# Output product from high and low parts, and a new order of VectorE and ScalarE behind the edge loop of a graph and attention layer

## The reference, cut to what matters

```python
m = v * attn[..., None]
out = jax.ops.segment_sum(m, dst, num_segments=n).reshape(n, H * D)
out = out @ Wo.T + bo
out = node_feat + out
mean, var = out.mean(axis=0), jnp.mean(jnp.square(out - mean), axis=0)
out = (out - mean) * jax.lax.rsqrt(var + EPS) * gamma + beta
...
kv = jnp.einsum('bhnd,bhne->bhde', kf, v)
z = jnp.einsum('bhnd,bhd->bhn', qf, kf.sum(axis=2))
out = jnp.einsum('bhnd,bhde->bhne', qf, kv) / (z[..., None] + EPS)
y @ w_proj + b_proj
...
x = x + gnn(xn, ...) + mix(xn)
x = x + ffn(_layernorm(x))
```

## Time and profile before

| | |
|---|---|
| median of 3 runs | 1625.43 us (1623.97 to 1627.98) |
| profiled execution | 1634.06 us, its span 1632.3 us |
| TensorE busy | 1547.8 us, 95% of the span |
| VectorE busy | 1253.1 us, 77% |
| ScalarE busy | 1053.7 us, 65% |
| GpSimd busy | 692.7 us, 42% |
| granted TensorE clock, mean | 0.985 of full speed |

### The profile page before, as it was taken

The page is one execution under the profiler, slowest core; times in us unless marked ns, Lnnn a source line. Parts: engine busy times, 40 slices in busy tenths (PEclk is TensorE's granted clock), DMA queues, the critical chain, the costliest instruction groups (busy, mean ns, idle before and its releaser), DMA issues. The chain is left out here.

```text
span 1632.3 us, 27290 instructions
## 1 busy us (share of the span) xinstructions
PE 1547.8 (95%) x7330; PEld 1200.3 (74%) x7334; DVE 1253.1 (77%) x3141; ACT 1053.7 (65%) x3706; POOL 692.7 (42%) x722
## 2 busy tenths in 40 slices
PE   7999897999999999999999999999999999999996
PEld 6886676777777777777777777777777776777663
DVE  5877654777787888888888778887888787678877
ACT  4775122667777777777777777777777776567244
POOL 1001123455555556555555565555555554211001
PEclk9999999999999999999999999999999999999997
DMA  5574415566666666666676666666676665175101
GB/s 193 182 242 180 178 64 154 179 214 194 213 204 208 228 210 216 208 201 197 205 237 214 206 214 204 214 208 204 213 219 207 201 211 175 54 226 178 37 14 51
DMA packets 135446, 300.31 MB, mean 184 GB/s; under 512 B 34863, under 2 KB 56502, under 8 KB 135296
## 3 DMA queue, kind: packets, MB, share of 16 engines
q0 software_dynamic: 63600, 180.17, 33.1%
q1 hardware_dynamic: 66512, 107.59, 22.2%
q10 hardware_dynamic: 5184, 10.81, 1.7%
HBM read 271.40 MB, written 66.58 MB: 207 GB/s over the span
## 5 line engine op out<-in xcount | busy, mean ns | idle before, releaser
L1110 ACT ACTIVATE wv<-vv,expd 128x64 f32<-128x64 f32 x1248 | 314.5, 334 | 2.8
L1122 ACT ACTIVATE old<-old,expd 128x64 f32<-128x64 f32 x1232 | 302.1, 334 | 0.0
L1032 POOL DMA_INDIRECT merge<-new,put_id x157 | 162.4, 1035 | 280.7 <-DVE new L1455 247.2
L1884 PE MATMUL psK<-M_hi,efT_hi 128*128 128x512 f32 x628 | 253.6, 404 | 2.8 <-ACT efT_hi L1080 2.8
L1884 PE MATMUL psV<-M_hi,efT_hi 128*128 128x512 f32 x628 | 255.9, 407 | 0.0
L1885 PE MATMUL psV<-M_lo,efT_hi 128*128 128x512 f32 x628 | 249.7, 398 | 0.0
L1885 PE MATMUL psK<-M_lo,efT_hi 128*128 128x512 f32 x628 | 249.2, 397 | 0.0
L1003 POOL DMA_INDIRECT old<-merge,dst_id x157 | 158.6, 1010 | 139.3 <-DMA merge<-new,put_id 109.2
L1096 ACT ACTIVATE expd<-diff 128x32 f32<-128x32 f32 (+1 forms) x79 | 18.1, 229 | 293.5 <-DVE diff L1434 293.5
L1003 POOL DMA_INDIRECT kv<-kv_table,src_id x157 | 160.7, 1023 | 66.1 <-issue 47.4
L1003 POOL DMA_INDIRECT qc<-q_table,dst_id x157 | 154.9, 987 | 55.7 <-issue 46.6
(11 more groups left out here) (323 smaller groups left out, 3323.5 us busy)
## 6 DMA issues: line engine op xcount, KB each, us to landing
first_ef<-in_ef_turned_dram SPq DMA_DIRECT2D x39, 512.0 KB
efT<-in_ef_turned_dram SPq DMA_DIRECT2D x39, 512.0 KB
merge<-empty ACTq DMA_DIRECT2D x4, 2640.0 KB, 9.7
rows<-merge SPq DMA_DIRECT2D x40, 256.0 KB, 3.8
row_block<-dst_rows POOLq DMA_DIRECT2D x13, 768.0 KB, 5.9
dst_line<-dst_rows SPq DMA_DIRECT2D x78, 128.0 KB
end_line<-end_rows SPq DMA_DIRECT2D x78, 128.0 KB
kv_table<-kv_out SPq DMA_DIRECT2D x10, 512.0 KB, 3.2
```

What stands on the lines that cost most here:

```text
L1032: pool.indirect_dma_start(out=merge[2 * (p % 2) + u][:, :], out_offset=bass.IndirectOffsetOnAxis(ap=put_id[:, t:t + 1], axis=0), in_=new[p ...
L1110: act.activation(wv[:, u, h * DH:(h + 1) * DH], vv[p % 2][:, u, h * DH:(h + 1) * DH], ACT.Copy, scale=expd[p % 2][:, u, 0, h:h + 1]).then_ ...
L1122: act.activation(rows, rows, ACT.Copy, scale=expd[p % 2][:, u, 1, h:h + 1]).then_inc(old_scaled, 1)
L1884: pe.matmul(out[:, :], efT_hi[b][:, u, c, :], Me_hi[:, c, col:col + D], start=c == 0, stop=False)
```

## The change

1. **Output product.** `Wo` and the transposed `g` are split into high and low parts in float32r, and each plain product of `output` becomes three products. The high part of `g` is made by `copy_g`, the low part by a new VectorE subtraction `turned_g_low` at the head of tile t for tile t-3. The high part of `Wo` is made by ScalarE at the end of its tile 8, the low part in two halves on VectorE in tiles 8 and 9. `turn_g` and `output` now wait for the low part.
2. **Place for them.** The scaled tables are written over `rows`; `part` is gone. SP may load the rows of tile t only when `g` of tile t-2 is made.
3. **VectorE's tile.** `add_parts` of tile t-1 moves from the end of tile t to its head, ahead of the minimum `before_exp`.
4. **ScalarE's tile.** `copy_v(t)` moves from the head of tile t+1 into the middle of tile t, between the two scaled tables.
5. **Division.** ScalarE takes the upper four heads of y (`weigh_half`), VectorE the lower four. In ScalarE's program `weigh_half(t+1)` stands ahead of `copy_y(t)`.
6. **Last stage.** On ScalarE `row_sd` goes ahead of `whole_numbers`, and `scale_y` goes behind it, one round later.

```diff
         wsc = sb("wsc", [P, 2, 2])
+        with ExitStack() as over_output:
+            Wo_lo = sb("Wo_lo", [P, C, D], F32R, where=over_output)
         Wo = sb("Wo", [P, C, D])
         with ExitStack() as over_queries:
...
+            with ExitStack() as over_ternary:
+                Wo_hi = sb("Wo_hi", [P, C, D], F32R, where=over_ternary)
             w_ffn = sb("w_ffn", [P, 2, 2 * D], where=sums_only)
...
-            sp.dma_start(Wo[:, :, :], WoT.rearrange("(c p) o -> p c o", p=P)).then_inc(Wo_in, 16)
+            sp.dma_start(Wo[:, :, :], WoT.rearrange("(c p) o -> p c o", p=P)).then_inc(w_in, 16)
             for t in range(2, NT):
-                sp.wait_ge(part0_done, 2 * (t - 1))
-                sp.wait_ge(act_parts, 2 * H * (t - 1))
-                sp.wait_ge(pool_part, t - 1)
+                sp.wait_ge(g_done, t - 1)
                 load_rows(t)
             sp.wait_ge(v_done, NT)
...
-                                   bc(scl2[:, t, 3, :], DH), ALU.mult).then_inc(pool_part, 1)
+                of_heads = rows[:, u, 3, :].rearrange("p (h e) -> p h e", e=DH)
+                pool.tensor_tensor(of_heads, of_heads, bc(scl2[:, t, 3, :], DH), ALU.mult).then_inc(pool_part, 1)
             pool.wait_ge(v_done, NT)
             pool.memset(res[:, NT - 1, :], 0.0).then_inc(cst, 1)
...
 
-            def parts(t):
+            def scale_table(t, i):
                 u = t % 2
                 act.wait_ge(scaled, 1 if t < 2 else 2)
                 act.wait_ge(rows_in[u], 16 * (TABLES + 1) * (t // 2 + 1))
-                if t >= 2:
-                    act.wait_ge(g_done, t - 1)
-                for i in (1, 2):
-                    for h in range(H):
-                        act.activation(part[:, u, i, h * DH:(h + 1) * DH], rows[:, u, i, h * DH:(h + 1) * DH], ACT.Copy,
-                                       scale=scl2[:, t, i, h:h + 1]).then_inc(act_parts, 1)
+                for h in range(H):
+                    of_head = rows[:, u, i, h * DH:(h + 1) * DH]
+                    act.activation(of_head, of_head, ACT.Copy, scale=scl2[:, t, i, h:h + 1]).then_inc(act_parts, 1)
 
             def copy_v(t):
...
             for t in range(NT):
-                if t >= 1:
-                    copy_v(t - 1)
                 exp(len(QJ) + t, D)
                 if t == 1:
                     table_exp(1)
-                parts(t)
+                scale_table(t, 1)
+                copy_v(t)
+                scale_table(t, 2)
                 if t >= 2:
                     copy_g(t - 2)
-            copy_v(NT - 1)
+                if t == 8:
+                    act.wait_ge(w_in, 64)
+                    act.wait_ge(summed_w, 5)
+                    act.activation(Wo_hi[:, :, :], Wo[:, :, :], ACT.Copy).then_inc(w_high, 1)
             copy_g(NT - 2)
             act.wait_ge(kv_added, NT)
...
             act.wait_ge(cst, 4)
+            def weigh_half(t):
+
+                u = t % 2
+                act.wait_ge(z_done, t + 1)
+                act.wait_ge(g_turned, NT)
+                if t >= 2:
+                    act.wait_ge(y_turned, t - 1)
+                for h in range(H // 2):
+                    act.activation(y[:, u, (H // 2 + h) * DH:(H // 2 + h + 1) * DH], ob[u][1][:, h * HW:h * HW + DH], ACT.Copy,
+                                   scale=z[:, t, 1, H // 2 + h:H // 2 + h + 1]).then_inc(y_half, 1)
+
+            weigh_half(0)
             for t in range(NT):
+                if t + 1 < NT:
+                    weigh_half(t + 1)
                 copy_y(t)
                 if t % 3 == 0:
...
+                if i < NT:
+                    row_sd(i)
                 if 0 <= i - 1 < NT:
                     whole_numbers(i - 1)
-                if i < NT:
-                    row_sd(i)
+                if 0 <= i - 3 < LAST:
+                    scale_y(i - 3)
                 if 0 <= i - 1 < NT:
...
                     copy_h(i - 2)
-                    if i - 2 < LAST:
-                        scale_y(i - 2)
 
...
-                dve.tensor_tensor(part[:, u, 0, :].rearrange("p (h e) -> p h e", e=DH),
-                                  rows[:, u, 0, 0:D].rearrange("p (h e) -> p h e", e=DH),
-                                  bc(scl2[:, t, 0, :], DH), ALU.mult).then_inc(part0_done, 1)
+                of_heads = rows[:, u, 0, :].rearrange("p (h e) -> p h e", e=DH)
+                dve.tensor_tensor(of_heads, of_heads, bc(scl2[:, t, 0, :], DH), ALU.mult).then_inc(part0_done, 1)
 
             def own_part(t):
...
-                dve.scalar_tensor_tensor(part[:, u, 0, :], v2[:, u, :], has[:, t, 0:1], part[:, u, 0, :],
+                dve.scalar_tensor_tensor(rows[:, u, 0, :], v2[:, u, :], has[:, t, 0:1], rows[:, u, 0, :],
                                          ALU.mult, ALU.add).then_inc(part0_done, 1)
 
             def add_parts(t):
                 u = t % 2
                 dve.wait_ge(act_parts, 2 * H * (t + 1))
-                two = mark(dve.tensor_tensor(part[:, u, 1, :], part[:, u, 1, :], part[:, u, 2, :], ALU.add))
+                two = mark(dve.tensor_tensor(rows[:, u, 1, :], rows[:, u, 1, :], rows[:, u, 2, :], ALU.add))
                 dve.wait_ge(pool_part, t + 1)
                 dve.wait_ge(part0_done, 2 * t + 2)
-                three = mark(dve.tensor_tensor(part[:, u, 0, :], part[:, u, 0, :], part[:, u, 3, :], ALU.add))
+                three = mark(dve.tensor_tensor(rows[:, u, 0, :], rows[:, u, 0, :], rows[:, u, 3, :], ALU.add))
                 dve.wait_ge(step, two)
                 dve.wait_ge(step, three)
                 if t >= 2:
                     dve.wait_ge(g_turned, t - 1)
-                dve.tensor_tensor(g[:, u, :], part[:, u, 0, :], part[:, u, 1, :], ALU.add).then_inc(g_done, 1)
+                dve.tensor_tensor(g[:, u, :], rows[:, u, 0, :], rows[:, u, 1, :], ALU.add).then_inc(g_done, 1)
+
+            def turned_g_low(t):
+                dve.wait_ge(gT_done, t + 1)
+                dve.tensor_tensor(gT_lo[:, :, t * P:(t + 1) * P], gb[:, :].rearrange("p (c e) -> p c e", c=C),
+                                  gT_hi[:, :, t * P:(t + 1) * P].bitcast(F32), ALU.subtract).then_inc(gT_low, 1)
+
+            def output_low(i):
+                half = slice(i * C // 2, (i + 1) * C // 2)
+                dve.wait_ge(w_high, WO + 1)
+                dve.tensor_tensor(Wo_lo[:, half, :], Wo[:, half, :], Wo_hi[:, half, :].bitcast(F32),
+                                  ALU.subtract).then_inc(w_low, 1)
 
             def queries_min(j):
                 before_exp(j, QJ[j][2], q_done, j + 1)
...
             table_maxima(0)
             for t in range(NT):
+                if t >= 1:
+                    add_parts(t - 1)
+                if t >= 3:
+                    turned_g_low(t - 3)
                 before_exp(len(QJ) + t, D, k_done, t + 1)
...
                     weight_sums()
                 if t == 5:
                     weight_scales()
                 if t in (6, 7):
                     ternary(t - 6)
+                if t >= 8:
+                    output_low(t - 8)
             add_parts(NT - 1)
+            turned_g_low(NT - 3)
 
             def weigh(t):
                 u = t % 2
...
+                dve.wait_ge(z_done, t + 1)
                 dve.wait_ge(g_turned, NT)
                 dve.wait_ge(kv_added, NT)
                 if t >= 2:
                     dve.wait_ge(y_turned, t - 1)
-                for i in range(2):
-                    dve.tensor_tensor(y[:, u, i * 256:(i + 1) * 256].rearrange("p (h d) -> p h d", d=DH),
-                                      heads[i][:, :, 0:DH], bc(z[:, t, 1, 4 * i:4 * i + 4], DH), ALU.mult).then_inc(y_scaled, 1)
+                dve.tensor_tensor(y[:, u, 0:D // 2].rearrange("p (h d) -> p h d", d=DH),
+                                  heads[0][:, :, 0:DH], bc(z[:, t, 1, 0:H // 2], DH), ALU.mult).then_inc(y_scaled, 1)
 
             dve.wait_ge(col_in, 64)
             column = mark(dve.tensor_tensor(col[:, 2, :], col[:, 2, :], col[:, 3, :], ALU.add))
...
             whole_x(0)
+            turned_g_low(NT - 2)
+            turned_g_low(NT - 1)
             for j, (c, k, n0, nn) in enumerate(OJ):
...
-                    pe.wait_ge(gT_done, t)
+                    pe.wait_ge(gT_low, t)
                 for c in range(C):
...
-                if t >= 2:
-                    pe.wait_ge(y_scaled, 2 * (t - 1))
+                pe.wait_ge(v_copied, NT + 2 * C)
+                if t >= 2:
+                    pe.wait_ge(y_scaled, t - 1)
+                    pe.wait_ge(y_half, H // 2 * (t - 1))
                 for c in range(C):
                     last = pe.matmul(ob[t % 2][c // 2][:, (c % 2) * PAIR:(c % 2 + 1) * PAIR],
...
                 if j >= R:
                     pe.wait_ge(oT_done, j - R + 1)
+                to, here = ring[j % R][:, 0:nn], slice(n0, n0 + nn)
                 for k in range(C):
-                    last = pe.matmul(ring[j % R][:, 0:nn], Wo[:, k, c * P:(c + 1) * P], gT[:, k, n0:n0 + nn],
```

(8 more changed lines are left out.)

71 lines of the change are left out of this document (31 added, 40 removed).

## The result

The changed kernel takes 1648.08 us (median of 4 executions, 1647.5 to 1648.92), the kernel before 1626.23 us beside it: ratio 1.0130, 95% interval 1.0117 to 1.0144. It is slower by 21.9 us. The forecast was 1644, with 1631 to 1653 as its range.

What follows compares the result with a forecast made beforehand. TensorE was taken to pace node tiles and output before the change, a VectorE-ScalarE ring the node tiles after it. Terms 15.0 + 0.75 + 2.2 + 0.5 = 18.4 us on 1625.4 gave 1644 us, range 1631 to 1653.

Steps and rivals of the forecast that it cites:

- minimum 0 to minimum 9: Node tiles, from VectorE's minimum of tile 0 to that of tile 9: 15.0 us longer, 11.1 without meetings.
- The ring: Node tiles: minimum, ScalarE's exponential and scalings, VectorE's additions, `g`, low part, next minimum take 8.26 us a tile.
- The meeting: Node tiles: GpSimd's multiplication and VectorE's additions hold each other up, 0.65 us more a tile, bounds 0 and 1.0.
- Rival (a): Node tiles: the rings hold but GpSimd and VectorE miss each other; 11 us slower, 1636 us; chance 0.25.
- The way to the second chunk: From tile 9's minimum to the output's second chunk: 0.75 us more, 0.6 of it for TensorE's lower clock; bounds 0 and 3.
- The loop: Output's loop: ScalarE's multiplications and `copy_y` lengthen VectorE's way from z by 0.91 us; 2.2 us more overall, bounds -5 and +5.
- The last stage: Last stage: GpSimd's sum meets VectorE's scaling of `hid`, partly offset at the end; 0.5 us more, bounds -3.3 and +2.5.
- Rival (b): Node tiles and output: TensorE stays the bound in both, so the kernel gets faster, 1614 us; chance 0.06.
- Rival (c): Node tiles: TensorE's waits keep its clock low, seven tiles cost up to 28 us more, 1672 us; chance 0.05.

Runs made afterwards that it cites:

- e3: Changed kernel with GpSimd's multiplication of tile t waiting for `g` of tile t-1, so after VectorE's additions: 1642.8 us, kernel before 1626.4 beside it.
- e1: Changed kernel with VectorE's minimum of tile t put ahead of the additions of tile t-1 and the low part of `g`: 1638.3 us, kernel before 1626.4.
- e2: Changed kernel with ScalarE's `copy_y(t)` put ahead of `weigh_half(t+1)` in the output stage: 1640.8 us, kernel before 1626.4 beside it.
- e9: Changed kernel with the division's sharing undone, VectorE multiplying both halves of y: 1641.8 us, kernel before 1625.9 beside it.
- e4: Changed kernel without the product of `Wo`'s low part with `g`'s high part, 8 matmuls a chunk instead of 12: 1646.2 us, kernel before 1626.4.
- e12: e8 with the last tile's keys-times-values ahead of the first output chunk, a later wait for `Wo`'s second low half, old last-stage order: 1626.86 us, ratio 1.0005.
- e13: e12 with VectorE's division directly behind the chunk's statistics and the second weight sum moved to tile 4: 1625.87 us, ratio 0.9992 to the kernel before.
- e8: Changed kernel with the edits of e1 and e2, and both halves of `Wo`'s low part taken in tile 9: 1639.4 us, kernel before 1637.3.
- e10: e8 with the division wholly on VectorE in place of ScalarE's copy first: 1634.3 us, kernel before 1625.9 beside it.

## Why the prediction was right

By its own terms, each beside what the same two instructions show in the profile after:

| term | predicted | measured |
|---|---|---|
| minimum 0 to minimum 9 | +15.0 | +16.08 (67.27 to 83.35) |
| minimum 9 to the second output chunk | +0.75 | +1.48 (10.81 to 12.29) |
| second chunk to the first turning back | +2.2 | +2.00 (53.83 to 55.83) |
| last stage | +0.5 | +0.88 (69.34 to 70.22) |
| sum | +18.4 | +20.4; medians +21.9 |

**The ring** was right in kind and size. Predicted 8.26 us a tile without meetings; e3 shows 8.28. Tile 0 was to take 8.71 and took 8.74, tile 1 8.4 and 8.47, tile 8 11.7 and 11.70. e1 shows that it was this ring that held the tiles: with the additions out of it 12.06 of the 16.08 us are back. Of the 4.0 that are left 3.6 lie between the minima of tiles 8 and 9 (9.39 us, 5.80 before), where VectorE waits for the high part of `Wo`.

**The meeting** was there and was undersized, 0.65 taken and 0.80 measured a tile (9.07 against 8.28), inside the bounds of 0 and 1.0. Six of them make 0.9 of the 1.08 us by which the first term fell short. The first addition came 5.68 us after the minimum, as worked out; GpSimd came 5.58 after it (1466.36 against 1460.78) and not 5.4, and so held the addition 0.18 longer. In three tiles it came 5.71 to 5.74 after it, just behind the start of the first addition, and held the second: 0.84 a tile. In the two in which it came latest (6.94 and 6.52) it held the addition into `g`: 0.77 and 0.68. That a slightly later landing costs more and not less stood in the prediction as a remark, and so it was, by 0.05; it should have gone into the sum. Rival (a) is what e3 made: 1642.8 us and not 1636, since (a) had also taken 3 off the last stage, and no order of the last stage that was run shows that.

**The way to the second chunk** is the term furthest off, by a factor of two, inside its bounds. The step that was mis-sized is the clock: 0.6 us was taken for some 3.5 us at the lower level. TensorE stood 4.14 and 2.67 us, as foreseen, but nearly the whole of the first chunk ran at the lower level (1512.73 to 1517.2), 2.1 us more than at the upper one. Part of that lies beside the chain over the low parts of `g`: at full clock the transpose of tile 8 (1518.55) would still have had to wait for the low part of tile 7, done at 1517.1. So I estimate from these rows that 1.3 of the 2.1 reached the second chunk; without them the way is 11.0, and the prediction had 10.95.

**The loop** came out by its chain, piece by piece: 3.20 us to VectorE's round 1, 3.61 for it, 40.75 for rounds 2 to 9 with the low parts of the projection's weights, 8.27 to the first turning back, where the working had 3.25, 3.6, 41.0 and 8.2. The wait of 1.02 us for `yT_hi` in nine tiles is what the 0.91 of the working stood for. e2 and e9 remove it, and gain 4.7 us. That TensorE's 6.2 us go into waiting holds too: of some 9 us more, e4 got 3. What the prediction did not see is that the cure was one line away. It named the multiplications on ScalarE as the cost; it was their place.

**The last stage** came near its term by luck. By kind it went as summed: GpSimd's sum starts 1.80 us after the quantisation, and against the kernel before six rounds of e1 cost 1.75 us more (1.5 predicted) and its end 1.6 less (1 predicted), which leaves 0.1. The other 0.73 of the 0.88 are the fall of the clock ahead of the second round, which no part of the sum stood for.

**Rival (b)**, TensorE remains the bound and the kernel gains 11 us, did not happen in the changed kernel; e12 and e13 come near it in kind. Even then the gain is 1 to 2 us in the sum of the stretches and none in the medians. In e12 the loop, from the second chunk to the first turning back, takes 49.14 us (1504.25 to 1553.39), 4.7 less than before the change: most of the 6.2 us of the product. But 1.5 us are given back in the node tiles (68.79 against 67.27) and 2.1 on the way to the second chunk (12.90 against 10.81). New there are VectorE's ten low parts of `g` and two of `Wo` (6.0 and 2.3 us of its time) and loads that come later; which of them takes how much wasn't tried. **Rival (c)** did not happen: over the tiles the clock is 0.97, as before the change.

Not tried: a third buffer for `rows`, which would take the ring of the loads away, since SBUF would have to be laid out anew for it. That e1's loads would set the pace of a still faster stage is therefore only argued. Nor was anything tried on why the clock falls in one execution and not in another of the same code.

## What to carry to other kernels

Before an instruction is put at the head of an engine's round, follow what it waits for back to the work of the same round on that engine: if the way comes back, the way's length is the round, whatever the busy shares say. Work handed to another engine goes behind what others wait for there, not ahead of it; the same handed-over multiplication cost 4.6 us or gained at most 1 by its place in a list. And ahead of a stage in which TensorE is the bound, shorten its wait and give it its small leftover products in it: in e12 that paid twice, by the wait and by the clock that did not fall. Last, before a difference of 1 us between two traces is explained, compare the granted clock in the stretch where it arises.

## What the runs showed of the hardware

- Where VectorE and GpSimd meet, they hold each other up in turn within one tile: VectorE's first addition (0.69) ran, GpSimd took 1.53 us for its 1.04, and VectorE's second addition then 1.53 for its 0.68. The cost is nearly the same, 0.79 or 0.84 us, whether GpSimd begins 0.10 before the first addition or 0.03 to 0.06 after its start. Where it came at the last addition, it was 0.68 to 0.77.
- VectorE's scaling of `hid` has one SBUF input, and is stretched like the additions with two: 1.24 us for 0.35, beside a sum of GpSimd begun 0.22 before it. The Trainium skill, in the section named above, counts `tensor_scalar` among the operations that can enter a 2-port mode and then contend with GpSimd; this row agrees.
- TensorE's granted clock was 0.50 in the 5 us in which it waited 2.67 after a wait of 4.14, and 0.58 in the next five, busy throughout. In e8 one wait of 3.66 gave 0.61 over the chunk behind it; in e12, with a wait of 0.63 in its place, it stayed at 1.00.
- The same code and the same waits can give another clock. The wait of 3.66 us ahead of the first chunk came in e8 and in e10; the chunk took 4.42 us in e8 and 5.29 in e10, which ran it at 0.50 throughout. A wait of 2.13 us in the last stage was followed by 0.68 over that round in the changed kernel and by 1.00 in e1 and e2.
